# Mask bias as one 128x128 identity product per bank; ones rows, byte masks and contexts in fewer transfers

## The chip, the cores and the metric

The kernel runs on one core of a Trainium2 chip. The metric is device time in microseconds (us) for one execution, as the median of several. TensorE (PE) multiplies, VectorE (DVE), ScalarE (ACT) and GpSimd (POOL) do the rest, and SyncE (SP) and ScalarE issue most DMA transfers. All engines run on their own and meet at semaphores.

## What is computed

Two transformer-like layers on 4 batches of 256 tokens with 128 features, each batch with a context of 512 keys. What matters here is the second layer's cross-attention with 16 heads of 8 features:

```
x = x + L0_xattn(layernorm(x), ctx, mask_bool)      # 2 heads of 64
x = x + L0_ffn(layernorm(x))
x = x + L1_xattn(layernorm(x), ctx, ctx, mask_int)  # 16 heads of 8
x = x + L1_ffn(layernorm(x))                        # 8 experts, one for each token

# L1_xattn
scores = einsum('bhsd,bhtd->bhst', qh, kh) / sqrt(8)
scores = where(mask == 0, -1e9, scores)
out    = einsum('bhst,bhtd->bhsd', softmax(scores), vh)
```

## The kernel before

The program is one instruction stream for each engine, with an order written out by hand in tables (`EARLY_AT`, `LATE_AT`, `BESIDE1`, `BESIDE2`). It has three stages. The first (to about 87 us of the profiled span) is the first layer's attention and gated network, beside the projections of the second layer. The second (87 to 228 us) is the second layer's attention, 16 units u (4 batches b of 4 groups of 4 heads j), with the first layer's leftovers beside it. The third is the experts.

In a unit of the second stage TensorE computes for each head j the scores twice: once by query (`scores_q`, line 1297, two products of 128x512), from which VectorE takes the row maximum (line 1048), and once by key (`scores_k`, line 1372, four products of 128x256 into two banks of PSUM), which ScalarE exponentiates (line 753, 128x1024 at a time). The probabilities of the unit before are then multiplied by the values (`weigh`, line 1386, behind j = 0 and j = 1). The products by query and by key both contract over 80 rows: 72 rows of bf16 parts and 8 rows in which the keys carry ones and the queries carry the negated maximum. Those ones come from `select_dram`, which `keys_back` (line 414) and `queries_out` (line 422) copy in.

Before the scores by key are summed into their banks, the banks get the mask bias (0, or a large negative number where the mask is 0). For 31 of the 64 pairs (u, j), where `biased(u, j)` is true (j = 2, and j = 3 but in the last unit), ScalarE writes the bias by a copy (`set_bias`, line 763). For the other 33 pairs, j = 0 and j = 1 of each unit and one more, TensorE adds it as a product with the identity (line 1367). That product is cut into four of 64x64, one for each quarter of the 128x128 array: rows 0 to 63 or 64 to 127 of the bias against the same rows of the identity, to columns 0 to 63 or 64 to 127 of the output. Two quarters fill the first bank straight, the other two fill the second bank crosswise, so its bias is stored with its halves swapped. The host lays `mask1k_dram` out so, VectorE makes the bias from it (`c1k`, line 914, semaphore `m1k_conv`), and `masks_straight` (line 437) copies the two swapped key tiles of a batch by DMA, in two halves of 64 partitions, to columns KT.. of `m1kb`, where ScalarE finds them unswapped (semaphore `m1k_straight`). These eight copies go through SP's queue, the first four behind `keys_out(2)`, the others between `keys_out(3)` and `keys_back(2)`.

`keys_out(b)` (line 409) writes the bf16 parts of the keys to DRAM, `keys_back(b)` reads them in the layout of the scores, and `queries_out(b)` (lines 422, 425, 429) does both for the queries. `batch_in(b)` on TensorE waits for all transfers of a batch. The regions are reused: the second half of `k_region` first holds both masks as integers.

At the start of the program SP issues the input transfers: tokens, constants, weights, contexts by batch (`context`, line 391), integer masks. ScalarE issues the byte masks of the first layer as four transfers (`masks_in`, line 653). VectorE converts the byte mask of batch 0, GpSimd those of batches 1 to 3 (line 523). Line 1198 is the first layer's key projection.

## Time and profile before

| | |
|---|---|
| median of 3 runs | 294.4 us (292.73 to 294.68) |
| the profiled execution | 295.71 us, of which 293.7 us span |
| mean granted TensorE clock | 0.935 |
| PE busy | 252.2 us, 86% |
| PE weight loads | 131.1 us, 45% |
| DVE busy | 188.1 us, 64% |
| ACT busy | 163.9 us, 56% |
| POOL busy | 105.3 us, 36% |

The span is the time from the first to the last instruction. Busy time is that of instructions recorded on an engine. A matmul's recorded end is modelled, so the distance from one start to the next tells more than its length. "Granted clock" 1.00 is 2.4 GHz, 0.50 is 1.2 GHz. The chain of work that ended last is followed back from the last instruction; its shares tell which engine set the time.

### The profile page before, as it was taken

The page shows a single profiled execution, that of the slowest core. Times are in us where ns is not written, and L with a number is a line of the kernel's source. Part 1 is how long each engine was busy: PE and PEld are TensorE (multiplying, and loading weights), DVE is VectorE, ACT ScalarE, POOL GpSimd, SP SyncE. Part 2 cuts the span into 40 slices and gives each one's busy share as a digit, 9 for nine tenths or more (in the row PEclk, how much of TensorE's full clock was granted, in tenths as well). Part 3 has the DMA queues.
Part 4 walks back from the last instruction along what each step waited for, and adds up shares of the span by engine and source line. Part 5 has one row for each costly group of instructions (what it writes and reads, how often), then busy time and mean ns, then how long its engine had stood idle before and what let it go on. Part 6 is the DMA issues. An engine that isn't in the chain of part 4 may idle for free.

```text
span 293.7 us, 5742 instructions
## 1 busy us (share of the span) xinstructions
PE 252.2 (86%) x1924; PEld 131.1 (45%) x1924; DVE 188.1 (64%) x662; ACT 163.9 (56%) x304; POOL 105.3 (36%) x124
## 2 busy tenths in 40 slices
PE   0799999698498999999999999999879889759991
PEld 0335657466263345444444443444443345425550
DVE  3191875947978777778879968789921267324340
ACT  1167475415026487887777887877765433333440
POOL 2542683611612421004321313113552514655533
PEclk9999999959897599999999999999986999968997
DMA  6990456342263769930003999621611761677400
GB/s 179 388 428 27 102 135 154 80 125 80 62 156 98 163 187 280 274 99 27 2 0 101 319 410 337 162 77 38 229 55 54 215 228 59 205 222 198 168 20 7
DMA packets 21451, 45.15 MB, mean 154 GB/s; under 512 B 1798, under 2 KB 16525, under 8 KB 20464
## 3 DMA queue, kind: packets, MB, share of 16 engines
q1 hardware_dynamic: 9936, 31.11, 33.6%
q10 hardware_dynamic: 9824, 10.00, 12.7%
q0 software_dynamic: 1664, 3.69, 3.8%
q8 instruction: 16, 0.26, 0.4%
q14 instruction: 11, 0.09, 0.1%
HBM read 30.85 MB, written 13.93 MB: 152 GB/s over the span
## 4 chain that ended last, share of the span: by engine, by line
PE 45%; DVE 9%; ACT 7%; issue 3%; another core or an unknown queue 3%; POOL 1%; POOLq 0%; DVEq 0%; ACTq 0%
PE banks L1386 10%; PE banks L1372 8%; PE banks L1297 7%; PE banks L1434 6%; DVE scores_unused L1048 6%; PE banks L1367 3%; ACT p_region L753 3%; PE banks L1464 2%; ACT banks L763 2%; PE banks L1162 2%; PE banks L1168 1%; PE banks L1453 1%; ACT ctx_region L744 1%; PE banks L1445 1%
## 5 line engine op out<-in xcount | busy, mean ns | idle before, releaser
L1048 DVE CUSTOM_DVE_ANT_0 scores_unused<-banks,mask_bias 128x512 bf16<-128x512 f32 x128 | 82.5, 688 | 15.7 <-PE banks L1297 14.7
L753 ACT ACTIVATE p_region<-banks 128x1024 f32<-128x1024 f32 x64 | 65.2, 1021 | 32.6 <-PE banks L1372 32.0
L1297 PE MATMUL banks<-k_region,q_region 80*128 80x512 bf16 x128 | 43.3, 403 | 5.1 <-DVE max L1048 4.3
L1372 PE MATMUL banks<-q_region,k_region 80*128 80x256 bf16 x256 | 40.9, 285 | 0.6 <-ACT banks L763 0.6
L605 POOL COPY q_region<-q_region 8x768 bf16<-8x768 bf16 x16 | 13.0, 814 | 68.6 <-ACT q_region L737 68.6
L1386 PE MATMUL banks<-p_region,values 128*9 128x256 f32 x512 | 35.4, 397 | 0.0
L511 POOL TENSOR_TENSOR ln_rstd<-ln_var_eps,minus_half 128x2 f32<-128x2 f32 x16 | 12.2, 764 | 59.8 <-DVE ln_var_eps L848 59.8
L763 ACT ACTIVATE banks<-mask_bias_by_key 128x1024 f32<-128x1024 bf16 x31 | 31.8, 1025 | 0.8
L1372 PEld LDWEIGHTS banks<-q_region,k_region 80*128 80x128 bf16 x256 | 22.8, 100 | 17.3 <-issue 10.8
L1434 PE MATMUL banks<-k_region,q_region 128*64 x64 | 24.0, 495 | 4.5 <-ACT q_region L777 4.3
L770 ACT ACTIVATE q_region<-banks 128x352 f32<-128x352 f32 x16 | 7.4, 463 | 30.5 <-PE banks L1435 22.2
L1435 PE MATMUL banks<-k_region,q_region 128*64 128x352 f32 x64 | 24.1, 496 | 0.0
L641 POOL DMA_INDIRECT out_dram<-q_region x16 | 15.9, 995 | 18.2 <-DVE q_region L1149 14.7
L1297 PEld LDWEIGHTS banks<-k_region,q_region 80*128 80x128 bf16 x128 | 11.1, 101 | 25.3 <-DVE max L1048 15.5
L1162 PE MATMUL banks<-constants,token_rows 128*128 128x128 f32 x32 | 7.1, 307 | 12.9 <-DVE token_rows L854 12.3
L596 POOL DMA_INDIRECT q_region<-binned_dram,mask_bias x16 | 15.7, 981 | 6.1 <-issue 4.2
L1386 PEld LDWEIGHTS banks<-p_region,values 128*9 128x9 f32 x512 | 11.2, 92 | 14.9 <-issue 8.4
L1137 DVE SCALAR_TENSOR_TENSOR q_region<-q_region,banks 128x352 f32<-128x352 f32 x16 | 8.3, 520 | 14.8 <-ACT q_region L770 13.3
L588 POOL DMA_INDIRECT binned_dram<-token_rows,mask_bias x8 | 8.2, 1028 | 22.3 <-issue 22.3
L1464 PE MATMUL banks<-k_region,q_region 128*64 (+1 forms) x96 | 14.6, 290 | 1.1 <-DVE q_region L1149 1.1
L1465 PE MATMUL banks<-k_region,q_region 128*64 128x128 f32 (+1 forms) x96 | 14.6, 290 | 0.0
L1367 PE MATMUL banks<-mask_bias_by_key,ident_bf 64*64 64x512 bf16 x132 | 14.4, 426 | 0.1
(151 smaller groups left out, 453.6 us busy)
## 6 DMA issues: line engine op xcount, KB each, us to landing
binned_dram<-ctx_region ACTq DMA_DIRECT2D x2, 4626.0 KB, 26.5
k_region<-experts_dram SPq DMA_DIRECT2D x17, 544.0 KB, 3.6
k_region<-k_parts_dram SPq DMA_DIRECT2D x4, 1152.0 KB
k_region<-experts_dram SPq DMA_DIRECT2D x1, 3808.0 KB, 19.1
q_region<-q_parts_dram SPq DMA_DIRECT2D x12, 192.0 KB
k_region<-mask1k_dram SPq DMA_DIRECT2D x1, 2048.0 KB, 11.5
k_region<-mask_dram SPq DMA_DIRECT2D x1, 2048.0 KB, 15.7
k_parts_dram<-q_region SPq DMA_DIRECT2D x4, 384.0 KB, 2.6
```

The lines of the kernel that those rows point to most:

```text
L596: g.indirect_dma_start(gin[:, s, :], None, bins_d[ph], bass.IndirectOffsetOnAxis(ap=row_at[:, s:s + 1], axis=0))\
L641: g.indirect_dma_start(out_d, bass.IndirectOffsetOnAxis(ap=gin[:, s - 1, 2 * D:ROW].bitcast(U32), axis=0), yo[:, (s - 1) % YBUFS, :], None ...
L753: a.activation(pt[:, u % 2, j, :, :].rearrange("p (c t) q -> p c (t q)", c=2), ps[:, c:c + 2, :], ACT.Exp, scale=float(D1) ** -0.5).then_i ...
L763: a.activation(ps[:, c:c + 2, :], m1kb[:, b, 2:6, :].rearrange("p (c t) q -> p c (t q)", c=2), ACT.Copy).then_inc(bias_set, 1)
L1048: return v.tensor_tensor_reduce(out=junk[:, q, :], in0=scores, in1=m1b[:, QT * (u // 4) + q, :], scale=1.0, scalar=-3e38, op0=ALU.add, op1 ...
L1297: return m.matmul(out, qst[0:R, (u * GH + j) * SQ + q * P:(u * GH + j) * SQ + (q + 1) * P], kst[0:R, (u * GH + j) * SK:(u * GH + j + 1) * ...
L1367: m.matmul(ps[o, first + c, :], identB[r, r], m1kb[r, b, 2 - 2 * c:4 - 2 * c, :].rearrange("p t q -> p (t q)"), start=True, stop=False, sk ...
L1372: last = m.matmul(ps[:, first + c, t * SQ:(t + 1) * SQ], kst[0:R, k:k + P], qst[0:R, (u * GH + j) * SQ:(u * GH + j + 1) * SQ], start=False ...
L1386: last = m.matmul(half(f"W{u}")[32 * j:32 * j + VW, :], v1[:, b * KT + t, u % 4 * GH + j, :], pt[:, u % 2, j, t, :], start=t == 0, stop=t ...
L1434: m.matmul(ps[0:HALF, to, 0:I], ginT[:, n % 2, 0:HALF], first, start=True, stop=True)
L1435: last = m.matmul(ps[HALF:P, to, 0:I], ginT[:, n % 2, HALF:P], second, start=True, stop=True)
L1464: m.matmul(ps[0:HALF, 6, 0:P], hT[0:rows, n % 2, c - HALF:c], first[0:rows], start=k == 0, stop=k == 2)
```

## The change

- The bias product becomes one 128x128 identity product for each bank: two products of 128x512 in place of four of 64x512, for each of the 33 pairs.
- The bias is stored straight, 4 key tiles in place of 6. The host's layout of `mask1k_dram` is plain. `masks_straight` and its eight DMAs are gone. `set_bias` waits for `m1k_conv` alone.
- The ones over the keys come in two transfers of two batches each, in place of four. The second, which also covers the region of the integer masks of batch 3, waits for `m1k_conv` of all batches before `keys_back(2)`. The same wait ahead of `keys_back(3)` is gone.
- The byte masks of batches 1 to 3 come in one transfer, the contexts of batches 2 and 3 in one.

```diff
@@ masks_in (ACT)
-                act.dma_start(m0u[:, b * QT * SK:(b + 1) * QT * SK], m0_d[:, b * QT * SK:(b + 1) * QT * SK]).then_inc(m0_in[b], 16)
+                n = 1 if b == 0 else B - 1
+                act.dma_start(m0u[:, b * QT * SK:(b + n) * QT * SK], m0_d[:, b * QT * SK:(b + n) * QT * SK]).then_inc(m0_in[b], 16)
@@ SP
-            context(2)
-            context(3)
+            context(2, 2)
@@ keys_back(b)
-                sp.dma_start(k_raw[0:MROWS, b * 4096:(b + 1) * 4096].rearrange("p (u n) -> p u n", u=GROUPS),
-                             sel_d[0:MROWS, :].unsqueeze(1).broadcast_to([MROWS, GROUPS, GH * SK // 2])).then_inc(k_in[b], 16)
+                if b % 2 == 0:
+                    if b:
+                        sp.wait_ge(m1k_conv, B)
+                    sp.dma_start(k_raw[0:MROWS, b * 4096:(b + 2) * 4096].rearrange("p (u n) -> p u n", u=2 * GROUPS),
+                                 sel_d[0:MROWS, :].unsqueeze(1).broadcast_to([MROWS, 2 * GROUPS, GH * SK // 2])).then_inc(k_ones_in[b // 2], 16)
@@ SP
-            masks_straight(0)
-            masks_straight(1)
...
-            masks_straight(2)
-            masks_straight(3)
             keys_back(2)
             arrived(sp, f"PV{B - 1}")
             queries_out(1)
-            sp.wait_ge(m1k_conv, B)
             keys_back(3)
@@ mask0(t) (POOL)
-                pool.wait_ge(m0_in[t // QT], 16)
+                pool.wait_ge(m0_in[1], 16)
@@ set_bias(u, j) (ACT)
-                    act.wait_ge(m1k_straight[b], 32)
+                    act.wait_ge(m1k_conv, b + 1)
@@ scores_k(u, j) (PE)
                     for c in range(2):
-                        for half in range(2):
-                            r = slice(64 * half, 64 * (half + 1))
-                            o = slice(64 * (half ^ c), 64 * ((half ^ c) + 1))
-                            m.matmul(ps[o, first + c, :], identB[r, r], m1kb[r, b, 2 - 2 * c:4 - 2 * c, :].rearrange("p t q -> p (t q)"),
-                                     start=True, stop=False, skip_group_check=True)
+                        m.matmul(ps[:, first + c, :], identB, m1kb[:, b, 2 * c:2 * c + 2, :].rearrange("p t q -> p (t q)"), start=True, stop=False,
+                                 skip_group_check=True)
```

How it moves instructions on TensorE, at j = 0 and j = 1 of a unit of the second stage, where the unit before is multiplied by its values. Before:

```order
L1297 MATMUL banks<-k_region,q_region 128x512 x2
L1367 MATMUL banks<-mask_bias_by_key,ident_bf 64x512 x4
L1372 MATMUL banks<-q_region,k_region 128x256 x4
L1386 MATMUL banks<-p_region,values 9x256 x8
L1297 MATMUL banks<-k_region,q_region 128x512 x2
```

And now (line 1297 is 1288, 1367 is 1356, 1372 is 1361 and 1386 is 1375 there):

```order
L1288 MATMUL banks<-k_region,q_region 128x512 x2
L1356 MATMUL banks<-mask_bias_by_key,ident_bf 128x512 x2
L1361 MATMUL banks<-q_region,k_region 128x256 x4
L1375 MATMUL banks<-p_region,values 9x256 x8
L1288 MATMUL banks<-k_region,q_region 128x512 x2
```

Nothing else moved there: the four quarter products became two whole ones in the same place.

On SP, at the passage from the first stage to the second, from the writing of the keys of batch 2. Before:

```order
L409 DMA k_parts_dram<-q_region 128x3x512 [waits k_split]
L437 DMA mask_bias_by_key<-mask_bias_by_key 64x512 [waits m1k_conv,m1_conv]
L437 DMA mask_bias_by_key<-mask_bias_by_key 64x512
L437 DMA mask_bias_by_key<-mask_bias_by_key 64x512 [waits m1k_conv]
L437 DMA mask_bias_by_key<-mask_bias_by_key 64x512
L414 DMA k_region<-select_dram 8x4x1024 [waits k_wr]
L416 DMA k_region<-k_parts_dram 72x1x8192
L422 DMA q_region<-select_dram 8x2x1024 [waits place_full_A]
L425 DMA q_parts_dram<-q_split_parts 128x3x256 [waits q_split]
```

And now (409 is 408, 414 is 416, 416 is 418, 422 is 424, 425 is 427):

```order
L408 DMA k_parts_dram<-q_region 128x3x512 [waits k_split]
L416 DMA k_region<-select_dram 8x8x1024 [waits m1k_conv,k_wr,m1_conv]
L418 DMA k_region<-k_parts_dram 72x1x8192
L424 DMA q_region<-select_dram 8x2x1024 [waits place_full_A]
L427 DMA q_parts_dram<-q_split_parts 128x3x256 [waits q_split]
```

The first row is `keys_out(3)` in both. The four mask copies behind it are gone, and the keys of batch 2 stand directly behind it, with the mask semaphores on the ones' transfer.

## Rows read from the trace of the kernel before

**Rows 1.** The page: the chain that ended last, by engine and by line.
```profile
PE 45%; DVE 9%; ACT 7%; issue 3%; another core or an unknown queue 3%; POOL 1%; POOLq 0%; DVEq 0%; ACTq 0%
...
L1367 PE MATMUL banks<-mask_bias_by_key,ident_bf 64*64 64x512 bf16 x132 | 14.4, 426 | 0.1
```

**Rows 2.** Windows: length, then busy us (count) of each engine, clock, DMA.
```profile
core 0: us, PE busy (x) PEld busy (x) DVE busy (x) ACT busy (x) POOL busy (x), PEclk, DMA share, GB/s
92.00:102.40 10.40, 10.30 (x50) 4.03 (x51) 7.49 (x31) 5.17 (x6) 5.34 (x7) 0.51 0.54 127
102.40:218.00 115.60, 108.75 (x988) 50.36 (x988) 92.19 (x343) 91.91 (x120) 28.46 (x34) 1.00 0.55 165
218.00:224.70 6.70, 6.69 (x43) 3.01 (x47) 1.67 (x12) 3.45 (x5) 3.68 (x4) 0.52 0.21 59
```

**Rows 3.** Timeline of TensorE, full clock: start, length, line, shape, count.
```profile
169.51 0.60 PE L1297 MATMUL banks<-k_region,q_region 80*128 80x512 bf16 x2
170.05 0.41 PE L1367 MATMUL banks<-mask_bias_by_key,ident_bf 64*64 64x512 bf16 x4
170.39 0.61 PE L1372 MATMUL banks<-q_region,k_region 80*128 80x256 bf16 x4
170.93 1.05 PE L1386 MATMUL banks<-p_region,values 128*9 128x256 f32 x16
171.91 0.44 PE L1162 MATMUL banks<-constants,ctx_region 128*128 128x128 f32 x2
172.19 0.60 PE L1297 MATMUL banks<-k_region,q_region 80*128 80x512 bf16 x2
172.62 0.60 PE L1372 MATMUL banks<-q_region,k_region 80*128 80x256 bf16 x4
```

**Rows 4.** Timeline of TensorE, half clock (the first stretch of rows 2).
```profile
95.66 1.06 PE L1372 MATMUL banks<-q_region,k_region 80*128 80x256 bf16 x4
96.51 1.06 PE L1297 MATMUL banks<-k_region,q_region 80*128 80x512 bf16 x2
97.50 0.64 PE L1367 MATMUL banks<-mask_bias_by_key,ident_bf 64*64 64x512 bf16 x4
98.08 1.04 PE L1372 MATMUL banks<-q_region,k_region 80*128 80x256 bf16 x4
```

**Rows 5.** Line 1367 in two windows, 92 to 103 and 218 to 225.5 us.
```profile
L1367 PE MATMUL banks<-mask_bias_by_key,ident_bf x8: 553/594/632, 97.5 to 101.8; 64*64 64x512 bf16 x8
...
L1367 PE MATMUL banks<-mask_bias_by_key,ident_bf x8: 630/631/632, 219.3 to 223.1; 64*64 64x512 bf16 x8
```

**Rows 6.** Timeline of TensorE ahead of the first half-clock stretch.
```profile
91.48 0.39 PE L1297 MATMUL banks<-k_region,q_region 80*128 80x512 bf16 x1 [0.84 <-DVE max L1048]
92.09 0.61 PE L1297 MATMUL banks<-k_region,q_region 80*128 80x512 bf16 x1 [0.22 <-DVE max L1048]
```

**Rows 7.** Timeline of SP's queue.
```profile
59.51 2.49 SPq L437 DMA_DIRECT2D mask_bias_by_key<-mask_bias_by_key  x4
64.89 2.18 SPq L429 DMA_DIRECT2D q_region<-q_parts_dram  x3
78.18 3.81 SPq L437 DMA_DIRECT2D mask_bias_by_key<-mask_bias_by_key  x4
82.56 0.84 SPq L416 DMA_DIRECT2D k_region<-k_parts_dram  x1
93.22 2.13 SPq L429 DMA_DIRECT2D q_region<-q_parts_dram  x3
```

**Rows 8.** The first product with the queries on TensorE's weight loads.
```profile
71.30 0.10 PEld L1297 LDWEIGHTS banks<-k_region,q_region 80*128 80x128 bf16 x1 [0.35 <-issue]
```

**Rows 9.** Timeline at the start: ScalarE's mask transfers, first waits, and GpSimd's first mask.
```profile
0.74 1.88 ACTq L653 DMA_DIRECT2D q_region<-mask_dram  x4
9.00 2.05 PE L1198 MATMUL banks<-ctx_region,weights 128*128 128x512 f32 x2 [1.46 <-DMA ctx_region<-ctxT_dram]
11.10 3.95 POOL L523 TENSOR_SCALAR mask_bias<-q_region 128x512 bf16<-128x512 uint8 x2
```

**Rows 10.** Time from issue to landing of line 653 (least, median, most).
```profile
DMA to landing us min/median/max: 3.0/4.5/6.4
```

More of the change, by code:

```diff
@@ L312, in build @@
         ident_in, w0_in, w_in, c_in = sem("ident_in"), sem("w0_in"), sem("w_in"), sem("c_in")
-        ctx_in = [sem(f"ctx_in{b}") for b in range(B)]
-        m0_in = [sem(f"m0_in{b}") for b in range(B)]
+        ctx_in = [sem(f"ctx_in{b}") for b in range(B - 1)]
+        m0_in = [sem(f"m0_in{b}") for b in range(2)]
         m1_in, m1k_in = sem("m1_in"), sem("m1k_in")
@@ L322, in build @@
         m0_conv, m1_conv, m1k_conv = sem("m0_conv"), sem("m1_conv"), sem("m1k_conv")
-        m1k_straight = [sem(f"m1k_straight{b}") for b in range(B)]
         bias_set = sem("bias_set")
@@ L329, in build @@
         q_in = [sem(f"q_in{b}") for b in range(B)]
+        k_ones_in = [sem(f"k_ones_in{b}") for b in range(0, B, 2)]
         kact_done = sem("kact_done")
@@ L430, in queries_out @@
                                  scrQ[b].rearrange("j (d h) n -> d j (h n)", h=H1)).then_inc(q_in[b], 16)
-            def masks_straight(b):
-                sp.wait_ge(m1k_conv, b + 1)
-                for half in range(2):
-                    r, o = 64 * half, 64 * (half ^ 1)
-                    sp.dma_start(m1kb[o:o + 64, b, KT:, :], m1kb[r:r + 64, b, 0:2, :]).then_inc(m1k_straight[b], 16)
             keys_out(0)
@@ L701, in beside @@
                     emptied(a.activation(n3T[:, tokens(b)], half(job), ACT.Copy), job)
-            for b in range(B):
+            for b in range(2):
                 masks_in(b)
@@ L913, in beside @@
                     dve.wait_ge(m1k_in, 16)
-                    v.tensor_scalar(m1kb[:, b, 0:KT, :], m1ki[:, b, :, :], 0.0, -BIG, ALU.is_equal, ALU.mult).then_inc(m1k_conv, 1)
+                    v.tensor_scalar(m1kb[:, b, :, :], m1ki[:, b, :, :], 0.0, -BIG, ALU.is_equal, ALU.mult).then_inc(m1k_conv, 1)
                 if kind == "fm":
@@ L1300, in batch_in @@
             def batch_in(b):
-                pe.wait_ge(k_in[b], 32)
+                pe.wait_ge(k_ones_in[b // 2], 16)
+                pe.wait_ge(k_in[b], 16)
                 pe.wait_ge(q_in[b], 64)
@@ L1363, in scores_k @@
                     for c in range(2):
-                        for half in range(2):
-                            r = slice(64 * half, 64 * (half + 1))
-                            o = slice(64 * (half ^ c), 64 * ((half ^ c) + 1))
-                            m.matmul(ps[o, first + c, :], identB[r, r], m1kb[r, b, 2 - 2 * c:4 - 2 * c, :].rearrange("p t q -> p (t q)"),
-                                     start=True, stop=False, skip_group_check=True)
+                        m.matmul(ps[:, first + c, :], identB, m1kb[:, b, 2 * c:2 * c + 2, :].rearrange("p t q -> p (t q)"), start=True, stop=False,
+                                 skip_group_check=True)
                 for c in range(2):
```

13 lines of the change are left out of this document (6 added, 7 removed).

## The prediction

> **What bounds the kernel now.** I read the page's chain first: TensorE holds 45% of it, VectorE 9%, ScalarE 7% [rows 1]. The windows of the second stage agree. From 102.4 to 218 us TensorE is busy 108.75 of 115.60 us, VectorE 92.19 and ScalarE 91.91 [rows 2]. So TensorE paces most of the second stage, and what the change does to its stream is the first term. The bias products are 132 instructions, 33 sets of four, busy 14.4 us in all [rows 1]. There is also a clock. In two stretches, 92.0 to 102.4 and 218.0 to 224.7 us, it is granted at 0.51 and 0.52, that is at 1.2 GHz, and everywhere between them at 2.4 GHz [rows 2]. Ahead of the first stretch TensorE had twice waited for VectorE's maxima, once for 0.84 us [rows 6].
>
> **The bias products at full clock.** TensorE's timeline gives distances from start to start [rows 3]. With a set of quarters: the two products of line 1297 start at 169.51, the quarters at 170.05, line 1372 at 170.39. That is 0.54 + 0.34 = 0.88 us. Without one: line 1297 at 172.19, line 1372 at 172.62, so 0.43 us for two whole products of 512 columns, 0.215 each. The first pair takes 0.11 us more than the second because of what follows it. The quarters take 0.34, which is one pass of 0.215 and again 0.12 or so. Likewise line 1372 takes 0.54 ahead of line 1386, whose products are 9 columns wide, against 4 x 0.107 = 0.43 for its own columns. So each passage between shapes that use the array in different parts costs about 0.11 us, and a set of quarters causes two. The four quarters do run together, but two of these passages eat the pass that this saves. Of the new products I expect none, since lines 1297, 1356 and 1361 of the new kernel all use the array whole: 4 x 0.215 = 0.86 us in place of 0.88. That is 0.02 less for each of 29 sets, 0.6 us where TensorE paces.
>
> The Trainium skill, on the page "TensorEngine Tiling (Array Packing)", speaks against the change in one rule and for it in another. Under "Theoretical Speedup" it puts two short dimensions at up to 4x or more, by which four quarters are one pass and two whole products are two: 0.215 us more for each of 33 sets, 7.1 us. Under "Key Properties" it says that changing the tiling mode drains the TensorE, with no figure. The trace agrees with the second rule (the 0.11 us above), and this is what takes the first one's gain away.
>
> **The bias products at half clock.** Line 1372 ahead of line 1297 takes 96.51 - 95.66 = 0.85 us for its 1024 columns, so 0.425 for 512. The set itself: from 96.51 over 97.50 to 98.08, 1.57 us [rows 4]. New: 4 x 0.425 = 1.70, that is 0.13 more. Eight instructions in the first stretch and eight in the second are two sets each [rows 5], so 4 sets and +0.5 us. With the 0.6 us from above, the sum on TensorE is -0.1 us.
>
> Its bounds. Below: I know of nothing that would make the new pair shorter than its columns, so -0.6 us (no half-clock sets at all). Above: if the 0.11 us passages stay although the shapes agree (because they come from the weights or from the switch between operands), a set costs 0.86 + 0.22 = 1.08, +0.20 us or 33 x 0.20 = +6.6 us; if one of the two stays, +3.0 us. I take -0.1, since the pair at 172.19 goes over to line 1372 with other operands and other weights at no cost.
>
> **The mask copies and SP's queue.** The four copies of 78.18 take 3.81 us of SP, four at 59.51 take 2.49 [rows 7]. All are off the path. Without the first four, the queries of batch 0 go out a little sooner; their last transfer is issued by 64.89 + 2.18 = 67.07, and TensorE loads the first weights that need them at 71.30 behind other work, with 0.35 us of its own issue and no wait for a DMA [rows 8]. Sooner gives nothing. Without the other four, the keys of batch 2 (82.56) start up to 3.8 us sooner, and the queries of batch 1, which had to wait until 93.22 behind them [rows 7], also. Batch 1 begins with `scores_q` six heads before unit 4. A unit takes (218 - 87) / 15 = 8.7 us, so that is at about 109 us, 14 us after the last of those transfers is issued (95.35). Nothing waits for them today. Price if that cover were gone: nothing, as they only move forward. The wait for `m1k_conv` that moves ahead of `keys_back(2)` sits behind SP's wait for `m1_conv` of all batches, and VectorE makes both masks of batch 3 in a row, the keys' first. So it is over by then; queued behind it are the keys of batch 2, needed at some 2.5 units after batch 1. The larger ones' transfer writes 8 partitions for two batches at 34 us, needed at 71 us. ScalarE's shorter wait costs and gives nothing, its bias was ready long before.
>
> **The start.** TensorE's first key projection waits 1.46 us for the context of batch 0, until 9.00 [rows 9]. This is on the path. The four mask transfers were issued between 0.74 and 2.62 us and landed within 6.4 us at most [rows 9, 10], so by about 9. They share the DMA engines with that context. The change brings the same bytes, in rows three times as long, posted up to 0.9 us sooner. That can move 9.00 either way. It cannot gain more than the 1.46 us of wait, and I see no more than about 1 us of loss, since the bytes ahead of the context are the same. Fewer and longer rows for the same bytes speak for a small gain, the earlier posting for a small loss; I take -0.1, near the middle. GpSimd starts on batch 1's mask at 11.10 [rows 9]; the joined transfer, issued by 1.7, would have to take over 9.4 us instead of 6.4 to delay it. It is then GpSimd's reciprocal roots that are late next, for at most the same time. Contexts 2 and 3 are needed from about 24 us on.
>
> **Sum.** -0.6 + 0.5 - 0.1 = -0.2 us against the profiled execution's 295.71 us (its span of 293.7 and 2.0 around it), so 295.5. The median of the runs lies 1.3 us below that execution, so I forecast 294.4 - 0.2 = 294.2 us.
>
> **Rivals.**
>
> Forecast, even exchange: within 291.5 and 297.3 us, chance 0.77. For it: the starts of rows 3 and 4, and no removed wait on the path. Its own 8 in 10 is 292.5 to 295.8, because the runs before spread from 292.73 to 294.68 by themselves.
>
> Rival 1, the packing was worth more (slower): the passages of 0.11 us stay when the shapes agree. Place: between lines 1288, 1356 and 1361 of the new kernel at j = 0 and 1. Price: +3.0 us with one passage of two, 297.4, and up to 6.6 or 7.1 us with both, 301. It passes +1% from 0.09 us for each set on. For it: I infer the cause of the 0.11 us from three pairs of starts only. Against it: the same two lines follow each other at 172.19 without any. Chance 0.07. A further 0.04 for slower goes to the clock: one more stretch at half clock like the second, 6.7 us long [rows 2], costs at most its half, 3.3 us, 297.5.
>
> Rival 2, a half-clock stretch is gone (faster). The short waits ahead of 92 us [rows 6] could fall otherwise, as TensorE's stream has other lengths. Price: in the first stretch TensorE's 10.3 us would be 5.2, but VectorE has 7.49 us of work there [rows 2], so 10.4 - 7.5 = 2.9 us at most, 291.3; in the second 6.7 - 3.45 (ScalarE's work) = 3.2 us, 291.0. Against it: nothing in the change touches what TensorE waits for ahead of either. Chance 0.12, which counts the cases where a part of such a gain meets one at the start.
>
> Rival 3, the transfers are all that shows: the start ends up to 1.4 us sooner, 292.9. It lies within the forecast's range.
>
> **Numbers.** About 1% is what a measurement of this kernel can tell from no change. The predicted time is 294.2. The range, 291.8 to 297.0, leaves out most of both far cases. Faster by over 1% 0.12, within 1% 0.77, slower by over 1% 0.11.
>
> **What would show it.** In the new trace, line 1356 should start 0.43 us after line 1288 and line 1361 another 0.43 us later at full clock; 0.54 in either place is rival 1. At half clock they should be 0.85 and 0.85. Line 1356's busy time should be near 14 to 16 us for 66 instructions. The first wait for the context should still be 0.5 to 2.5 us. SP's transfer of the keys of batch 2 should start near 79 us, and TensorE should show no wait for a DMA at batch 1. The half-clock stretches should lie where they were; if their number or length differs, the time follows them and not the change. I would be wrong if the distance at full clock is over 0.95 us for the four, or if the start moves by more than 1.5 us.

## Result: 0.9% faster, where no change was forecast

| | before | changed |
|---|---|---|
| median | 293.49 us (290.27 to 296.79, 22 runs) | 290.68 us (288.83 to 295.64, 22 runs) |
| the profiled execution, its span | 295.71 us, 293.7 us | 290.37 us, 288.5 us |
| its mean granted TensorE clock | 0.935 | 0.958 |

The ratio of the medians is 0.990. The forecast was 294.2 us with a range of 291.8 to 297.0, so the result is within 1%, the case that had 0.77, and yet 1.1 us below the range. 0.9 us of the distance to the forecast is its baseline, 294.4 us from three executions, where 22 give 293.49. Over the executions within 1.5% of each kernel's fastest the ratio is 0.991, 95% interval 0.988 to 0.994, but medians here and below are over all executions, those at a low clock too, since how often the clock is low turned out to be what the change moves, and since on the first chip below that limit would leave 2 of 23 executions of the kernel before.

The page of the changed kernel first: the chain by engine, and the bias product (compare [rows 1]). TensorE's share fell, VectorE's rose. The product has 16.7 us for the 49 of its 66 instructions that were recorded.

```profile
PE 42%; DVE 12%; ACT 6%; issue 4%; another core or an unknown queue 3%; POOL 1%; POOLq 0%; DVEq 0%; ACTq 0%
...
L1356 PE MATMUL banks<-mask_bias_by_key,ident_bf 128*128 128x512 bf16 x49 | 16.7, 394 | 1.4 <-DVE max L1039 0.3
```

Its windows (compare [rows 2]): the same 10.4 us from 92.0 now pass at full clock, and TensorE does 76 instructions there in place of 50. The second stretch at half clock is there as before, 5 us earlier.

```profile
core 0: us, PE busy (x) PEld busy (x) DVE busy (x) ACT busy (x) POOL busy (x), PEclk, DMA share, GB/s
...
92.00:102.40 10.40, 9.51 (x76) 4.54 (x76) 9.38 (x33) 7.87 (x12) 6.49 (x9) 1.00 0.67 167
102.40:213.00 110.60, 103.02 (x884) 51.78 (x895) 88.33 (x331) 87.77 (x114) 27.20 (x33) 1.00 0.57 167
213.00:220.00 7.00, 6.72 (x38) 3.31 (x42) 1.68 (x12) 3.50 (x5) 3.70 (x4) 0.51 0.21 59
```

To see where the time went, I used ScalarE's 64 exponentials of the second stage as marks, since every kernel has them in the same order. The 1st, 7th, 58th and 63rd, from ScalarE's timeline of the kernel before:

```profile
87.79 1.02 ACT L753 ACTIVATE p_region<-banks 128x1024 f32<-128x1024 f32 x1 [1.22 <-PE banks L1372]
...
105.22 1.02 ACT L753 ACTIVATE p_region<-banks 128x1024 f32<-128x1024 f32 x1
...
213.63 1.02 ACT L753 ACTIVATE p_region<-banks 128x1024 f32<-128x1024 f32 x1 [0.32 <-issue]
...
227.93 1.02 ACT L753 ACTIVATE p_region<-banks 128x1024 f32<-128x1024 f32 x1
```

And of the changed one:

```profile
86.25 1.02 ACT L744 ACTIVATE p_region<-banks 128x1024 f32<-128x1024 f32 x1 [1.30 <-PE banks L1361]
...
100.46 1.02 ACT L744 ACTIVATE p_region<-banks 128x1024 f32<-128x1024 f32 x1
...
208.61 1.02 ACT L744 ACTIVATE p_region<-banks 128x1024 f32<-128x1024 f32 x1 [0.31 <-issue]
...
223.10 1.02 ACT L744 ACTIVATE p_region<-banks 128x1024 f32<-128x1024 f32 x1
```

| from, to | before | changed | difference |
|---|---|---|---|
| start to mark 1 | 87.79 | 86.25 | -1.54 |
| mark 1 to 7 | 17.43 | 14.21 | -3.22 |
| mark 7 to 58, full clock throughout | 108.41 | 108.15 | -0.26 |
| mark 58 to 63 | 14.30 | 14.49 | +0.19 |
| mark 63 to the end of the span | 65.77 | 65.40 | -0.37 |
| span | 293.7 | 288.5 | -5.2 |

Two rows carry it: the start, and the half-clock stretch behind mark 1 that is gone. The two profiled executions differ by 5.3 us where the medians differ by 2.8, because the first was one at the lowest clock of its kernel (0.935) and the second at a middling one (0.958, where the median over the 22 is 0.953).

The start, from the changed kernel's timeline (compare [rows 9]): TensorE's first key projection starts at 7.66 without a wait for its context, and GpSimd's first mask at 9.88.

```profile
0.74 0.97 ACTq L644 DMA_DIRECT2D q_region<-mask_dram  x2
...
7.66 2.05 PE L1189 MATMUL banks<-ctx_region,weights 128*128 128x512 f32 x2
...
9.88 3.95 POOL L513 TENSOR_SCALAR mask_bias<-q_region 128x512 bf16<-128x512 uint8 x2
```

### The profile page after: what moved, and what is told of

Same layout as the page of the kernel before. It is cut to its first block, busy times and chain, and to the rows that moved or that the text cites. A ratio compares the mean times of both kernels' runs of the same rounds, so it can differ in the third digit from the quotient of the medians.

```text
span 288.5 us, 5583 instructions
## 1 busy us (share of the span) xinstructions
PE 245.9 (85%) x1841; PEld 133.7 (46%) x1858; DVE 187.8 (65%) x662; ACT 163.8 (57%) x304; POOL 105.5 (37%) x124
## 4 chain that ended last, share of the span: by engine, by line
PE 42%; DVE 12%; ACT 6%; issue 4%; another core or an unknown queue 3%; POOL 1%; POOLq 0%; DVEq 0%; ACTq 0%
PE banks L1375 10%; DVE scores_unused L1039 6%; PE banks L1361 6%; PE banks L1288 6%; PE banks L1423 6%; PE banks L1356 4%; PE banks L1453 2%; ACT p_region L744 2%; ACT banks L754 2%; PE banks L1153 2%; PE banks L1442 1%; ACT ctx_region L735 1%; PE banks L1159 1%; PE banks L1434 1%
## 5 line engine op out<-in xcount | busy, mean ns | idle before, releaser
L1039 DVE CUSTOM_DVE_ANT_0 scores_unused<-banks,mask_bias 128x512 bf16<-128x512 f32 x128 | 82.5, 688 | 13.6 <-PE banks L1288 12.5
L1288 PE MATMUL banks<-k_region,q_region 80*128 80x512 bf16 x128 | 42.2, 392 | 5.8 <-DVE max L1039 5.0
L1361 PE MATMUL banks<-q_region,k_region 80*128 80x256 bf16 x256 | 39.3, 277 | 0.6 <-ACT banks L754 0.6
L1375 PE MATMUL banks<-p_region,values 128*9 128x256 f32 x512 | 34.3, 388 | 0.0
L501 POOL TENSOR_TENSOR ln_rstd<-ln_var_eps,minus_half 128x2 f32<-128x2 f32 x16 | 12.3, 766 | 57.1 <-DVE ln_var_eps L839 57.1
L1361 PEld LDWEIGHTS banks<-q_region,k_region 80*128 80x128 bf16 x256 | 25.0, 98 | 16.7 <-issue 2.9
L1356 PE MATMUL banks<-mask_bias_by_key,ident_bf 128*128 128x512 bf16 x49 | 16.7, 394 | 1.4 <-DVE max L1039 0.3
L1453 PE MATMUL banks<-k_region,q_region 128*64 (+1 forms) x96 | 13.9, 281 | 2.7 <-DVE q_region L1140 2.7
L1454 PE MATMUL banks<-k_region,q_region 128*64 128x128 f32 (+1 forms) x96 | 14.0, 281 | 0.0
```

What stands on the lines that cost most here:

```text
L1039: return v.tensor_tensor_reduce(out=junk[:, q, :], in0=scores, in1=m1b[:, QT * (u // 4) + q, :], scale=1.0, scalar=-3e38, op0=ALU.add, op1 ...
L1288: return m.matmul(out, qst[0:R, (u * GH + j) * SQ + q * P:(u * GH + j) * SQ + (q + 1) * P], kst[0:R, (u * GH + j) * SK:(u * GH + j + 1) * ...
L1356: m.matmul(ps[:, first + c, :], identB, m1kb[:, b, 2 * c:2 * c + 2, :].rearrange("p t q -> p (t q)"), start=True, stop=False, skip_group_c ...
L1361: last = m.matmul(ps[:, first + c, t * SQ:(t + 1) * SQ], kst[0:R, k:k + P], qst[0:R, (u * GH + j) * SQ:(u * GH + j + 1) * SQ], start=False ...
L1375: last = m.matmul(half(f"W{u}")[32 * j:32 * j + VW, :], v1[:, b * KT + t, u % 4 * GH + j, :], pt[:, u % 2, j, t, :], start=t == 0, stop=t ...
L1453: m.matmul(ps[0:HALF, 6, 0:P], hT[0:rows, n % 2, c - HALF:c], first[0:rows], start=k == 0, stop=k == 2)
```

## Experiments

Each experiment was timed against the kernel before on the same chip. Five chips took part. On three of them the kernel before runs near 287 us, on two near 293 to 294, as in the comparison above. Most of that distance lies behind mark 63: the last part takes 64.9 to 67.0 us there and 57.9 to 62.5 us elsewhere. So I compare within a chip. "Difference" is median less median of before on that chip, with a 95% interval by resampling; "clock" is the median of the executions' mean granted clock. The first four rows are of one chip, the next four of another, and so on; the last two are of the fifth.

| kernel | median us | difference us | clock, of before | runs |
|---|---|---|---|---|
| before_start | 285.05 | -2.1 [-3.9, +0.1] | 0.959, 0.951 | 6 |
| before_product | 283.17 | -3.9 [-5.3, -2.7] | 0.973, 0.951 | 12 |
| after_old_start | 284.70 | -2.4 [-4.9, -0.2] | 0.965, 0.951 | 6 |
| after_copies | 282.09 | -5.0 [-6.5, -2.6] | 0.972, 0.951 | 12 |
| after_again | 283.81 | -3.1 [-5.4, -1.0] | 0.966, 0.951 | 12 |
| before_first_whole | 286.91 | 0.0 [-5.0, +2.4] | 0.960, 0.951 | 12 |
| before_rest_whole | 284.84 | -2.1 [-4.4, +0.1] | 0.961, 0.951 | 12 |
| after_busy | 278.17 | -8.8 [-10.6, -6.6] | 0.988, 0.951 | 6 |
| before_busy | 284.11 | -2.3 [-4.8, +0.6] | 0.979, 0.957 | 12 |
| before_product_busy | 283.21 | -3.2 [-5.2, -1.5] | 0.980, 0.957 | 6 |
| after_busy_more | 278.52 | -7.9 [-10.2, -5.8] | 0.993, 0.957 | 6 |
| after_switch | 291.23 | +4.9 [+1.2, +8.2] | 0.962, 0.957 | 6 |
| after_quarters | 293.53 | +0.8 [+0.1, +2.4] | 0.936, 0.954 | 12 |
| after_thrice | 290.51 | -2.2 [-3.0, +0.7] | 0.953, 0.954 | 12 |
| after_busy_copies | 288.34 | -4.4 [-5.8, -3.6] | 0.978, 0.954 | 6 |
| after_busy_old_start | 285.76 | -7.0 [-8.1, -6.3] | 0.981, 0.954 | 6 |
| before_late | 294.23 | 0.0 [-1.3, +2.1] | 0.952, 0.946 | 12 |
| before_product_again | 290.66 | -3.6 [-5.4, -1.4] | 0.963, 0.946 | 6 |

**How time and clock go together.** On one chip the kernel before ran at 0.939 to 0.940 in 13 of 29 executions (287.8 to 289.3 us) and at 0.957 to 0.966 in 14 others (283.0 to 288.1 us). A straight line through the 29 gives 1.7 us for each 0.01 of clock; over the changed kernel's 22 runs it gives 1.6. So one program takes one of a few levels in each execution, and a difference of 0.02 in clock is worth some 3 us.

### The parts alone: start, product, copies

before_start joins the byte masks and contexts as the change does, on the kernel before:

```diff
-                act.dma_start(m0u[:, b * QT * SK:(b + 1) * QT * SK], ...
+                n = 1 if b == 0 else B - 1
+                act.dma_start(m0u[:, b * QT * SK:(b + n) * QT * SK], ...
...
-            context(2)
-            context(3)
+            context(2, 2)
```

> The kernel before with only the start changed: byte masks of batches 1 to 3 in one transfer, contexts of batches 2 and 3 in one. Theory S (the start): the first context lands sooner, TensorE's first key projection begins at about 7.7 us in place of 9.0, and the time falls by about 1.3 us, by 2 to 3 with a share from the clock; ratio 0.990 to 0.996. Theory P (the product): the start is worth little, ratio 0.998 to 1.002. Theory C (the copies): as P.

It gained 2.1 us, with an interval that reaches +0.1, and 0.0075 of clock would be 1.3 us of it. The direct part is in its profile: the key projection starts at 7.70 without a wait.

```profile
7.70 2.05 PE L1198 MATMUL banks<-ctx_region,weights 128*128 128x512 f32 x2
```

before_product changes the product only, on the kernel before (bias rows from the copies, which hold them straight):

```diff
+                    if u % 4 == 0 and j == 0:
+                        pe.wait_ge(m1k_straight[b], 32)
...
-                        for half in range(2):
...
+                        m.matmul(ps[:, first + c, :], identB, m1kb[:, b, 2 + 2 * c:4 + 2 * c, :].rearrange("p t q -> p (t q)"), ...
```

> The kernel before with only the bias product changed: two whole identity products in place of four quarters, all transfers and the mask copies kept (the second bank's bias is read from the straight copies). Theory S: an even exchange, 0.88 us for a set either way, ratio 0.998 to 1.002, half-clock stretches as before. Theory P: most of the gain is here, ratio near 0.991, and fewer half-clock stretches because more of the array is at work.

This is the surprise: -3.9 us from an edit that saves 0.26 us of TensorE's time between marks 7 and 58 (108.41 to 108.15 us in its profile too, so 0.010 us for each of the 26 sets there). The rest is clock: 0.0215, at 1.7 us for each 0.01 some 3.7 us.

after_old_start is the changed kernel with four transfers of byte masks and four of contexts again, after_copies the changed kernel with `masks_straight` and its eight DMAs back at their old places in SP's queue.

> The changed kernel with the old start: four mask transfers, four context transfers. Theory S: the first key projection begins near 9.0 us again and nearly the whole gain is lost, ratio to before 0.997 to 1.001. Theory P or C: the gain stays, ratio near 0.991.

> The changed kernel with the eight mask copies put back in SP's queue at their old places, and ScalarE waiting for them; what they bring is not read. Theory S and P: nothing waits for them, ratio to before near 0.991 as the changed kernel. Theory C (SP's queue was the cost): the gain falls away, ratio near 1.000.

Against after_again's -3.1 us, the old start gave -2.4 and the copies gave -5.0. So no gain from removing the copies shows in the medians. It looks rather like a loss of 2 us, at a clock 0.006 lower, but between two chips and within the intervals, so I leave that open. The old start did not take the gain away, as it would have if the start were nearly all of it.

### Is it the form of the product or the moment?

Two theories stood: A, whole products keep the clock up by their form; C, any small shift in time re-deals the stretches. before_first_whole has whole products in units 0 and 1 alone (`if u < 2`), before_rest_whole in units 2 to 15 alone.

> The kernel before with whole identity products in units 0 and 1 alone (5 of 33 sets); 28 sets stay in quarters. Theory A (what TensorE does just ahead of 92 us decides the half-clock stretch at 92 to 102 us, and quarters there, which use a part of the array, let it fall): the stretch is gone or shorter, -1.5 to -3 us, the later stretches as in before. Theory B (the form anywhere in the second stage works by the load that the clock looks back on over a long time): little here, -0.5 us. Theory C (the clock falls by small shifts in time, whatever the form): any stretch may come or go, and the runs of one program spread over 0.02 of mean clock.

> The other half of that edit: quarters in units 0 and 1, whole products in units 2 to 15 (28 of 33 sets). Theory A: the stretch at 92 to 102 us stays as in before, and the gain is what the later stretches give, 0 to -1.5 us. Theory B: about -3.5 us, as with all 33 sets whole. Theory C: no difference to before_first_whole that follows from the place.

The place ahead of 92 us does not decide: before_first_whole kept its long stretch (90.2 to 100.4 us in its profile) although the two units' products were whole, and its runs spread from 0.939 to 0.987. Theory A in that narrow sense fell. More follows from it: its first quarter product starts at 105.94, behind that stretch, and up to there TensorE's stream is that of before_product, whose profile has no such stretch. So one and the same stream can have the stretch behind mark 1 or not, and the 3.22 us between marks 1 and 7 of the first pair can't be put down to the form. Each half of the edit gave about half of the clock, 0.0085 and 0.0095, but both intervals take in zero.

Over many profiles a difference by form is there all the same. Of the profiles without the filling products that come below, the four with all bias products in quarters (before, before_start, before_late, after_quarters) have 13.7 to 20.5 us at half clock between marks 1 and 63, and the seven with all of them whole and nothing added (the changed kernel's three, before_product's two, after_old_start, after_copies) have 3.4 to 10.2 us.

after_quarters turns the form alone back on the changed kernel, beside after_thrice, the changed kernel itself. It reads the straight bias crosswise in the second bank, so half of its masks fall on the wrong keys; the work is the same:

```diff
-                        m.matmul(ps[:, first + c, :], identB, m1kb[:, b, 2 * c:2 * c + 2, :].rearrange("p t q -> p (t q)"), ...
+                        for half in range(2):
+                            r = slice(64 * half, 64 * (half + 1))
+                            o = slice(64 * (half ^ c), 64 * ((half ^ c) + 1))
+                            m.matmul(ps[o, first + c, :], identB[r, r], m1kb[r, b, 2 * c:2 * c + 2, :].rearrange("p t q -> p (t q)"), ...
```

> The changed kernel with the identity products in quarters as before, everything else as changed; the second bank's bias is read from the straight copy, so the mask lands on the wrong keys there (the masking is wrong in that part, the work is the same). If the form of the product sets the granted clock: median clock back to 0.95 to 0.96, 2 to 4 us slower than the changed kernel, and most profiled stretches between 87 and 105 us and at 215 to 230 us longer. If only the timing does: clock as in the changed kernel, 0.966, and +0.3 us from the product itself (0.011 us a set).

> The changed kernel as it is, beside after_quarters on one chip. 283.8 us and clock 0.966, as on the chip of after_again.

The quarters cost 3.0 us [+0.1, +4.8] and 0.017 of clock [0.004, 0.026]. Both kernels missed their expected clocks: 0.936 and 0.953, in place of 0.95 to 0.96 and 0.966. On this chip the changed kernel's clock is no higher than that of the kernel before (0.954), and its -2.2 us has an interval that reaches +0.7. The granted clock on the two pages (40 slices of the span, tenths of full speed), after_quarters first:

```profile
PEclk9999999989597589999999999999986999968997
```

and after_thrice:

```profile
PEclk9999999979689799999999999999999999959996
```

With quarters the stretch behind mark 1 is 14 us long (91.6 to 105.3) and one at 218 to 225 us is added. Marks 1 to 7 took 18.77 us against 15.82. The changed kernel's own stretch behind mark 1, absent in its first profile, is here at 95.0 to 98.4 us, and at 96.1 to 99.5 in after_again.

after_quarters says one thing more. It has the form of the kernel before, and its clock is still 0.0185 lower [0.004, 0.025], its time 0.8 us longer. So the change's other parts moved the clock as much as the form did, and theory C isn't out.

before_late shifts the kernel before by loading the first tokens twice:

```diff
+            sp.dma_start(row[:, 0:QT, D:2 * D], rows_of(0)).then_inc(first_in, 16)
+            sp.wait_ge(first_in, 16)
             sp.dma_start(row[:, 0:QT, D:2 * D], rows_of(0)).then_inc(x_in[0], 16)
```

> The kernel before whose SP first loads the tokens of batch 0 once more and waits for them; all its own transfers follow 2 to 3 us later, ScalarE's mask transfers stay. If shifts in time decide the granted clock: another set of clocks than 0.94 to 0.966, up to 0.97 or more, or under 0.93. If the work of TensorE decides: the same clocks and 2 to 3 us more than before.

> The kernel before with whole identity products, on another chip than before_product. By the form: median clock at least 0.01 above before, 2 to 4 us faster. If before_product was the luck of its chip: within 1 us of before.

The shift came out as 0.64 us for the key projection (9.64, and no wait for the context there) and 0.61 at mark 1, not the 2 to 3 us expected, and neither time nor clock moved clearly. That is a weak test of shifts in time: all engines moved by about the same. The clock row of its page:

```profile
PEclk9999999959897599999999999999987999987998
```

and that of the kernel before, nearly the same pattern:

```profile
PEclk9999999959897599999999999999986999968997
```

before_product_again repeated the gain of the form on another chip: -3.6 us, +0.0165 of clock. So the form moves the clock in three comparisons of three in kernels with gaps; the small uniform shift didn't in one of one. Why four quarter products do it is open. Twice as many instructions and weight loads go with them, and that wasn't separated. The passages between array forms alone don't seem to do it: after_switch, next, has two in each set and ran at 0.962, where the kernel before had 0.957 beside it; the changed kernel was not timed on that chip.

### What a passage costs

```diff
+                        if c == 0:
+                            m.matmul(ps[0:64, first, 0:8], identB[0:64, 0:64], m1kb[0:64, b, 0, 0:8], start=True, stop=True)
                         m.matmul(ps[:, first + c, :], identB, ...
```

> The changed kernel with one tiny product of a 64x64 quarter (8 columns) in front of each of the 33 pairs of identity products; the pair then overwrites it. By the theory of the passages (0.11 us when the used part of the array changes, and again back), a set costs 0.22 us more, 7 us in all where TensorE paces, at equal clock. If the passages belong to something else (the weights, the operands), it costs the 8 columns and one more instruction, under 0.03 us each, 1 us in all.

Marks 7 to 58 took 113.76 us in place of 108.14, 5.6 us for 26 sets, 0.216 us each: twice 0.108. TensorE's timeline of after_switch:

```profile
133.01 0.60 PE L1288 MATMUL banks<-k_region,q_region 80*128 80x512 bf16 x2
133.55 0.19 PE L1357 MATMUL banks<-mask_bias_by_key,ident_bf 64*64 64x8 bf16 x1
133.67 0.60 PE L1358 MATMUL banks<-mask_bias_by_key,ident_bf 128*128 128x512 bf16 x2
134.11 0.60 PE L1363 MATMUL banks<-q_region,k_region 80*128 80x256 bf16 x4
```

0.54 ahead of the quarter in place of 0.43, 0.12 for its 8 columns, then 0.44. The prediction inferred this price from three pairs of starts; here it is measured by itself. TensorE's weight loads show where it goes, the whole pair of the changed kernel first, then the quarter of after_switch:

```profile
102.54 0.31 PEld L1356 LDWEIGHTS banks<-mask_bias_by_key,ident_bf 128*128 128x128 bf16 x2
...
133.55 0.10 PEld L1357 LDWEIGHTS banks<-mask_bias_by_key,ident_bf 64*64 64x64 bf16 x1 [0.42 <-issue]
```

Between whole products the weights are loaded during the product before, 0.21 us ahead of their own product at 102.75. At a change of form the load of 0.10 us starts together with its product, and nothing covers it. In the kernel before it is the same on the way back, behind quarters of 512 columns (load and product of line 1372 at 170.38 and 170.39), so the eight columns of after_switch are not the reason.

### TensorE kept busy

keep_busy is n products of the identity with a bias, into a bank that is free or written over next. They stand where TensorE has nothing to do:

```diff
+                    if b < 2:
+                        keep_busy(bank(job), (5, 14)[b])
                     pe.wait_ge(ln3_done, b + 1)
...
+                    if (u, j) in ((0, 1), (0, 2)):
+                        claim(pe, "vv2")
+                        keep_busy(bank("vv2"), (1, 3)[j - 1])
```

and 8 more in units 14 and 15.

> The changed kernel with identity products added (nothing reads their output) in stretches in which TensorE has nothing to do: 5 and 14 ahead of two waits of the first stage, 4 at the head of the second, 8 at its end. It adds 31 x 0.22 = 6.6 us of work off the path at full clock. If the half-clock stretches follow idle time of TensorE: those at 56 to 63, 76 to 80 and 213 to 220 us go or shrink, mean clock 0.97 or more, -2 to -5 us against the changed kernel. If they don't: same clock and 0 to +4 us.

> The kernel before with the same added identity products in TensorE's idle stretches as after_busy. If most of the difference between the two kernels came through the granted clock, both now run near 0.985 and this kernel ends 1 to 2 us behind after_busy, by the start alone. If the change is worth something besides (products, queue), it stays 3 us behind. And if the quarters themselves bring the clock down, this kernel still has half-clock stretches in the second stage where after_busy had none (clock 0.97 or less, 4 us or more behind).

> before_busy with all 33 identity products whole. With the clock held up in both, it shows the price of the product alone. Forecast by the distances in the traces (0.88 us a set in quarters, 0.86 whole): -0.7 us, within 1 us. If quarters bring the clock down by themselves: -3 us or more, with a clock 0.01 or more higher than before_busy. If the packing was worth something: +3 us or more.

> after_busy with 16 more identity products (3.4 us) in the wait of 3.5 us at 239.8 us, ahead of the second half of the experts. If idle time of TensorE is what the half-clock stretch at 242.5 to 246.5 us follows: it is gone, clock 0.99 or more, -1 to -2 us against after_busy; a release of the wait that is late by what the products run over costs up to 0.5 us of it. If not: same clock, same time or slower.

after_busy is the fastest kernel of the study: 5.6 us below the changed one on the same chip [3.9 to 6.8], 8.8 below the kernel before. It does 31 products more, which no result needs. The page of after_busy has one short stretch left ahead of the end:

```profile
PEclk9999999999999999999999999999999999979998
```

The Trainium skill, "TensorE: Matmul & The Clock Gate" under "HAM oscillation — how this bites in real kernels", says that a wait between bursts of products lets the clock fall; the trace agrees. That last stretch belongs to the one long wait that I had left empty, and starts in it, at 242.9:

```profile
243.28 0.45 PE L1441 MATMUL banks<-constants,q_region 128*128 128x128 f32 x1 [3.53 <-DMA q_region<-binned_dram,mask_bias]
```

after_busy_more fills it, and TensorE's timeline shows 3.47 us of products in its place, with the clock at 1.00 behind:

```profile
243.54 3.63 PE L1179 MATMUL banks<-mask_bias_by_key,ident_bf 128*128 128x512 bf16 x16
...
247.01 0.27 PE L1443 MATMUL banks<-constants,q_region 128*128 128x128 f32 x1
```

From mark 63 to the end it took 59.5 us against 61.2, as expected, but the median did not follow (278.5 us on another chip, -7.9 against -8.8): in its profiled execution a stretch at 91.9 to 95.3 us took 1.6 us back.

before_busy was a half miss. Its clock rose to 0.979, and it still stayed 5.6 us [3.5 to 8.4] behind after_busy_more on the same chip, not 1 to 2. Clock explains a part; at like clocks (0.985 to 0.991) its executions take 282.6 to 282.7 us and those of after_busy, on another chip, 276.6 to 278.6, some 4.5 us apart. before_product_busy says that this isn't mainly the product: -0.9 us [-3.2, +1.0] against before_busy, and no clear gain in clock (0.980 to 0.979). So with the gaps filled no effect of the form on the clock could be measured. Most of the 4.5 us had to come from elsewhere, by the change's other parts from the start and the queue.

### SP's queue, with its cover gone

TensorE's timelines at the first products with the queries, before_busy first:

```profile
67.65 1.02 PE L1208 MATMUL banks<-ctx_region,weights 128*128 128x512 f32 x2
71.45 1.86 PE L1304 MATMUL banks<-k_region,q_region 80*128 80x512 bf16 x4 [2.78 <-issue]
```

and after_busy:

```profile
64.81 1.02 PE L1199 MATMUL banks<-ctx_region,weights 128*128 128x512 f32 x2
66.92 1.02 PE L1295 MATMUL banks<-k_region,q_region 80*128 80x512 bf16 x4 [1.08 <-DMA q_region<-q_parts_dram]
```

TensorE waits 2.8 us for the queries with the mask copies ahead of them, and 1.1 us without. The profile of the kernel before shows no such wait, because a half-clock stretch at 57.8 to 64.7 us made TensorE late by as much. Where that stretch is 3.4 us long, the wait is there without any filling: 1.0 us in before_rest_whole and before_product_again, 1.3 us in after_copies, and none in the kernels without copies. The next two kernels put the copies, and the old start, back into after_busy.

> after_busy with the eight mask copies back in SP's queue. Theory of the hidden queue: the first scores by query wait 2.8 us instead of 1.1 us for their queries' transfer, so 1.5 to 1.8 us slower than after_busy (278.2), at the same clock. If the copies cost nothing (as the prediction had it): same time.

> after_busy with four transfers of byte masks and four of contexts again. Theory: the first key projection waits for its context again and everything follows 1 to 2 us later, 279.2 to 280.2 us. Together with the copies this would leave about 1 us of the 4.4 us between before_busy and after_busy. If the start costs nothing: 278.2 us.

The copies cost 2.6 us [+1.1, +3.9] between these two kernels, although after_busy_copies has the better start. Its timeline:

```profile
66.67 1.02 PE L1211 MATMUL banks<-ctx_region,weights 128*128 128x512 f32 x2
70.33 1.51 PE L1307 MATMUL banks<-k_region,q_region 80*128 80x512 bf16 x4 [2.63 <-DMA q_region<-q_parts_dram]
```

SP's queue in it:

```profile
58.08 0.37 SPq L409 DMA_DIRECT2D k_parts_dram<-q_region  x1
58.50 2.48 SPq L440 DMA_DIRECT2D mask_bias_by_key<-mask_bias_by_key  x4
...
63.89 2.18 SPq L432 DMA_DIRECT2D q_region<-q_parts_dram  x3
```

and in after_busy_old_start:

```profile
56.83 0.37 SPq L409 DMA_DIRECT2D k_parts_dram<-q_region  x1
...
60.97 2.10 SPq L432 DMA_DIRECT2D q_region<-q_parts_dram  x3
```

From the writing of the keys to the first product with the queries it is 70.33 - 58.08 = 12.3 us with the copies and 67.56 - 56.83 = 10.7 us without (67.56 is where that product starts in after_busy_old_start), so 1.5 us directly. (Every filled kernel agrees: 12.3 to 12.5 us in the three with copies, 10.7 to 10.8 in the three without.) A half-clock stretch also stands behind the longer wait, at 70.7 to 74.1 us in after_busy_copies, 71.4 to 74.8 in before_busy and 72.0 to 75.4 in before_product_busy, and none in the three without copies. The start is worth 0.9 to 1.8 us by the distance of after_busy (-8.8; after_busy_more -7.9) to after_busy_old_start (-7.0), and the copies 3.5 to 4.4 by the distance to after_busy_copies (-4.4). These two go across chips. They are enough for the 4.5 us, but one thing is not separated from them: how long the first products take twice their time differs between executions (last section) and is not in the clock column. after_busy and after_busy_more are the same up to 239 us, and neither profile has a half-clock stretch ahead of mark 1, yet it comes at 81.28 us in the one, where the doubled times ended sooner, and at 83.52 in the other.

## Why the prediction was wrong

**The product's own time: right.** The changed kernel's timeline at full clock gives 0.43 and 0.44 us, 0.87 for the four, where 0.86 was forecast:

```profile
102.32 0.60 PE L1288 MATMUL banks<-k_region,q_region 80*128 80x512 bf16 x2
102.75 0.60 PE L1356 MATMUL banks<-mask_bias_by_key,ident_bf 128*128 128x512 bf16 x2
103.19 0.60 PE L1361 MATMUL banks<-q_region,k_region 80*128 80x256 bf16 x4
103.72 0.62 PE L1375 MATMUL banks<-p_region,values 128*9 128x256 f32 x8
```

At half clock it is 219.00 - 218.14 = 0.86, forecast 0.85:

```profile
218.14 1.06 PE L1356 MATMUL banks<-mask_bias_by_key,ident_bf 128*128 128x512 bf16 x2
219.00 1.05 PE L1361 MATMUL banks<-q_region,k_region 80*128 80x256 bf16 x4
```

The 29 sets were put at 0.02 each; they brought 0.010. Rival 1 is out: no passage is left, and each costs the 0.11 us that was inferred. The Trainium skill's rule in "TensorEngine Tiling (Array Packing)" under "Key Properties", that a change of mode drains the engine, agrees with the 0.216 us for a change and back; the gain under "Theoretical Speedup" did not show in the time of a set (0.88 us in quarters, 0.87 whole), though the four quarters do run together.

**The step that failed: "nothing in the change touches what TensorE waits for ahead of either."** The sentence is true, and it was the wrong test. The waits ahead of the stretch are still there in the changed kernel, as long as in [rows 6]:

```profile
89.87 0.39 PE L1288 MATMUL banks<-k_region,q_region 80*128 80x512 bf16 x1 [0.85 <-DVE max L1039]
90.48 0.39 PE L1288 MATMUL banks<-k_region,q_region 80*128 80x512 bf16 x1 [0.22 <-DVE max L1039]
```

and yet the clock stayed at 2.4 GHz behind them in this execution. The prediction let the clock depend on waits alone and gave the product's form no part in it, so rival 2, which is what the profiled pair shows, got 0.12. Its price, 2.9 us at most for the first stretch, is near the 3.22 between marks 1 and 7, and that is in part luck: the changed kernel's other two profiles have 3.4 us of half clock there and take 15.8 us, not 14.21. The second stretch stayed in this profile and is gone in those two. What the form alone is worth through the clock, 3.6 to 3.9 us on the kernel before and 3.0 us on the changed one, was in no term of the sum. I had taken the half-clock stretches of one profiled execution for fixed places and not for one draw among several: over all executions the clock of the kernel before went from 0.935 to 0.972, with one at 0.99.

**The start: right mechanism, term mis-sized.** -0.1 us was taken, "near the middle" of -1.46 and +1. The profiled pair shows 9.00 - 7.66 = 1.34 us, GpSimd's mask 1.22 us sooner. Over all profiles with the usual order at SP, the key projection starts at 8.66 us on average with four mask transfers (9 profiles, 8.27 to 9.02) and at 7.80 with two (10 profiles, 7.58 to 8.36). So -0.9 us, with a spread of 0.8 us within each form. The remark that fewer and longer rows speak for a gain was right, and the sum should have followed it; the earlier posting cost nothing. "The first wait for the context should still be 0.5 to 2.5 us" failed in the changed kernel's profile, which has no such wait, though after_again's has one of 0.9 us.

**SP's queue: right for the execution shown, wrong on its cover.** The keys of batch 2 start at 76.94 (forecast near 79), the queries of batch 1 at 90.89, both sooner as said (from 82.56 and 93.22 [rows 7]), and TensorE waits for neither. But "Sooner gives nothing" held for the queries of batch 0 only because of the half-clock stretch at 57.8 to 64.7 us. Its margin was thin: in the kernel before the product with the queries starts at 71.61, and with the 12.3 us from above the queries were there at 59.08 + 12.3 = 71.4. "Price if that cover were gone" was asked for the keys of batch 2 and the queries of batch 1 and not for these; it is 1.5 us in the filled kernels, and at least the 2.6 us from above with the stretch that follows.

**The sum.** By the parts the change should have been worth more than it was: form 3.6 to 3.9, start 0.9 to 2.1, together 4.5 to 6, measured 2.2 to 3.1 us in three comparisons. What takes the difference back is not settled. The clock of the whole change (0.953 to 0.966) is below that of the form alone (0.963 to 0.973), and the one kernel with form, start and the old copies reached -5.0 us, so it goes through the clock too. On one chip after_quarters shows the same: all of the change but the form gave +0.8 us [+0.1, +2.4] and a clock 0.0185 lower, although the start and SP's queue are ahead in it. Which wait brings the clock down wasn't tried.

## What to carry to other kernels

Where a profile shows stretches at 1.2 GHz, treat them as a draw: look at the granted clock of many executions before pricing an edit by one of them, and give every edit of TensorE's stream, and of the transfers that it waits for, a chance of moving it. A stall that "nobody waits for" can be hidden by such a stretch; ask what it costs at full clock. And if TensorE has gaps, filling them with products that nobody reads is an edit worth trying before any finer one: 31 of them were worth 5.6 us here, about twice the change under study.

## What the runs showed of the hardware

- Four concurrent 64x64 products in place of two whole ones, equal in time to 0.010 to 0.015 us a set, lower the mean granted clock by 0.017 to 0.022 in a kernel with gaps, and by nothing that could be measured (0.0015, interval -0.003 to +0.0105) in one with its gaps filled.
- Between whole products TensorE loads weights during the product before (0.21 us ahead of their own). At a change between 64x64 and 128x128 products the load of 0.10 us is uncovered, and each change costs 0.11 us.
- At 7 to 15 us the products take twice their later time, though the granted clock is given as 1.00 there: two of 128x512 in f32 take 2.05 us at 7.66 and 1.02 us at 64.81. The trace of the changed kernel has no record of the clock ahead of 15.1 us, so the 1.00 says nothing there. In four profiles (before_start, before_first_whole, after_busy, after_busy_old_start) the first record is at 10.4 to 11.9 us, and ScalarE's first exponential starts 5.2 to 5.4 us behind the first key projection, against 6.1 to 6.2 us in the other sixteen.
- Two chips ran the last part, from mark 63 on, some 5 us slower than the others, whatever the kernel (64.9 to 67.0 against 57.9 to 62.5 us). Half of it is in one place: before_product and before_product_again are the same kernel, and there the second's TensorE falls 3.8 us behind within 1 us of work, by a wait of 3.7 us at its line 1433 (256.45), where the first's has none. A half-clock stretch of 6.9 us lies around it (253.6 to 260.5). What ends that wait late is not shown.
